# Reordering TensorE's turn in a pipelined LM block: dense products between the transposes, the scores and the scan products

## Time and profile before

| | |
|---|---|
| median of 3 runs | 1468.62 us (1467.59 to 1469.27) |
| the profiled execution | 1464.07 us, its span 1462.2 us |
| mean granted clock of PE | 0.915 |
| PE busy | 1184.4 us, 81% |
| DVE busy | 1160.4 us, 79% |
| ACT busy | 757.9 us, 52% |
| POOL busy | 819.6 us, 56% |
| HBM | 63 GB/s over the span |

### The profile page before, as it was taken

One profiled execution on the slowest core, in us unless ns is written; L12 is line 12 of the kernel. 1 busy time (PEld: TensorE's weight loads), 2 busy tenths in 40 slices (PEclk: granted clock), 3 DMA queues, 4 the chain that ended last, 5 costly groups with the idle time before them and its releaser, 6 DMA issues. The chain is left out here.

```text
span 1462.2 us, 25531 instructions
## 1 busy us (share of the span) xinstructions
PE 1184.4 (81%) x7199; PEld 814.6 (56%) x7206; DVE 1160.4 (79%) x2087; ACT 757.9 (52%) x1108; POOL 819.6 (56%) x2326
## 2 busy tenths in 40 slices
PE   0694043498989898989898989899999999898767
PEld 0352021357575756676767666666666675757444
DVE  4899933678888889888888989888888978878268
ACT  4667352354637373828273737473736555451247
POOL 7860027574757566575757575757575757560100
PEclk9999996599989899989899989998989989999889
DMA  9999400000001010101000000000000000000015
GB/s 367 408 407 425 160 23 16 12 19 16 23 10 31 1 32 3 30 6 26 10 22 16 16 16 16 16 16 16 16 16 16 16 16 16 18 17 1 0 42 188
DMA packets 62068, 92.22 MB, mean 63 GB/s; under 512 B 9101, under 2 KB 55010, under 8 KB 57554
## 3 DMA queue, kind: packets, MB, share of 16 engines
q1 hardware_dynamic: 58386, 82.10, 15.8%
q0 software_dynamic: 3072, 8.39, 1.5%
q10 hardware_dynamic: 576, 1.31, 0.2%
HBM read 81.29 MB, written 10.49 MB: 63 GB/s over the span
## 5 line engine op out<-in xcount | busy, mean ns | idle before, releaser
L747 POOL TENSOR_TENSOR stp<-Gs,X 128x32 f32<-128x32 f32 x1024 | 290.4, 284 | 263.1 <-ACT X L722 152.9
L749 POOL TENSOR_TENSOR Gs<-Gs,stp 128x32 f32<-128x32 f32 x1024 | 286.6, 280 | 80.3
L1048 PE MATMUL bank<-mT,w_fc 128*128 128x512 f32 x512 | 236.3, 599 | 7.9 <-ACT mT L1036 7.9
L604 PE MATMUL bank<-xT,w_in 128*128 128x512 f32 x512 | 235.8, 610 | 8.0 <-DVE uT L851 8.0
L1067 PE MATMUL bank<-w_fc,gl 128*128 128x256 f32 x1024 | 236.5, 379 | 0.0
L1067 PEld LDWEIGHTS bank<-w_fc,gl 128*128 128x128 f32 x1024 | 193.4, 190 | 59.8 <-issue 37.5
L837 ACT ACTIVATE uT<-bank,cols 128x512 f32<-128x512 f32 x64 | 49.5, 778 | 276.6 <-PE bank L604 276.6
L604 PEld LDWEIGHTS bank<-xT,w_in 128*128 128x128 f32 x512 | 97.7, 196 | 117.6 <-issue 107.1
L1048 PEld LDWEIGHTS bank<-mT,w_fc 128*128 128x128 f32 x512 | 95.7, 192 | 100.1 <-issue 94.7
L952 PE MATMUL bank<-MT,utok 128*64 128x128 f32 x1024 | 112.1, 408 | 45.5 <-DVE MT L938 45.4
L851 DVE SCALAR_TENSOR_TENSOR uT<-bank,cols,uT 128x500 f32<-128x500 f32 (+1 forms) x192 | 135.1, 736 | 3.0 <-ACT uT L837 0.7
(11 more groups left out here) (171 smaller groups left out, 1899.8 us busy)
## 6 DMA issues: line engine op xcount, KB each, us to landing
ring<-in_table SPq DMA_DIRECT2D x32, 1536.0 KB, 20.9
d_rep<-d_rows SPq DMA_DIRECT2D x128, 64.0 KB, 2.7
out<-res SPq DMA_DIRECT2D x16, 512.0 KB, 2.9
b_rep<-bc_rows SPq DMA_DIRECT2D x128, 32.0 KB, 1.8
c_rep<-bc_rows SPq DMA_DIRECT2D x128, 32.0 KB, 1.8
w_fc<-in_w_fc SPq DMA_DIRECT2D x2, 1024.0 KB, 8.8
w_in<-in_w_in ACTq DMA_DIRECT2D x1, 1088.0 KB, 5.2
h<-in_table,ids POOLq DMA_INDIRECT x64, 9.8
```

The source lines that it names most:

```text
L604: last = pe.matmul(dst, w_in[:, k, c0:c1], xT[:, k, :], start=(k == 0), stop=(k == KD - 1))
L747: pool.tensor_tensor(stp[:], Gs[:, t, ::-1, :], X2[:, t, :, :], ALU.mult).then_inc(rec.sem, 1)
L749: pool.tensor_tensor(Gs[:, t + 1, :, :], Gs[:, t, :, :], stp[:], ALU.add).then_inc(rec.sem, 1)
L1048: last = pe.matmul(pj[n % 4][:, :], w_fc1[:, k, n * P:(n + 1) * P], mT[:, k, :], start=(k == 0), stop=(k == KD - 1))
```

## The change

No arithmetic is changed. It moves pieces in PE's and DVE's orders, puts the scores in other banks, and splits `dve_gate`:

- PE: the transposes of u stand before tiles 5 and 6 of fc2, the first scores before tile 7. The four banks of scores are tb[0], tb[1], pj[2], pj[3], so the scores wait for the gate (`z_ready`) and for all of `gelu`, and the second head group's first pair waits for three masks in place of two (pj[2] must have been read). Tiles 0 and 1 of `pe_u` stand between the second scores and the second scan products, tiles 2 and 3 behind them. `pe_out` takes over the wait for `h2_ready`.
- DVE: `dve_layer_norm` goes from before `dve_inverse` to behind `dve_mean3`; `dve_row_stats` goes to before the first masks; `dve_h2` to behind them; `dve_stats3` to behind the gates; the skip of tiles 0 and 1 is before the second masks and their gate behind; the first half of the convolution is before `dve_bc`.

```
--- before.py
+++ after.py
@@ -822,8 +822,8 @@
                 dve.scalar_tensor_tensor(q, rm[:, :, hg * SC:(hg + 1) * SC].rearrange("p t s -> p s t"), DOWN80, q,
                                          ALU.mult, ALU.mult).then_inc(q_ready.sem, 1)
 
-        def pe_u(pe, g):
-            for f in range(UT):
+        def pe_u(pe, g, tiles):
+            for f in tiles:
                 if since(g):
 
                     pe.wait_ge(gate1.sem, gate1.at(g - 1, f + 1))
@@ -907,15 +907,16 @@
                 dve.scalar_tensor_tensor(xl[:, j, :], rows(g, j), rs1[:, bass.ds(g * G + j, 1)], out_b[:],
                                          ALU.mult, ALU.add).then_inc(xl_ready.sem, 1)
 
-        score_bank = (sbk[0], sbk[1], tb[0], tb[1])
+        score_bank = (tb[0], tb[1], pj[2], pj[3])
 
         def pe_scores(pe, g, hg):
             if hg == 0:
                 pe.wait_ge(k_ready.sem, k_ready.at(g))
                 pe.wait_ge(utok_ready.sem, utok_ready.at(g))
+                pe.wait_ge(z_ready.sem, z_ready.at(g))
                 if since(g):
 
-                    pe.wait_ge(h2_ready.sem, h2_ready.at(g - 1))
+                    pe.wait_ge(gelu.sem, gelu.at(g - 1))
             else:
                 pe.wait_ge(m_ready.sem, m_ready.at(g, 4))
             pe.wait_ge(q_ready.sem, q_ready.at(g, hg + 1))
@@ -940,12 +941,8 @@
                               ALU.mult).then_inc(m_ready.sem, 1)
 
         def pe_scan_out(pe, g, hg, pair):
-            if hg == 0 and pair == 0:
-
-                pe.wait_ge(z_ready.sem, z_ready.at(g))
-                if since(g):
-                    pe.wait_ge(gelu.sem, gelu.at(g - 1))
-            pe.wait_ge(m_ready.sem, m_ready.at(g, 4 * hg + 2 * pair + 2))
+
+            pe.wait_ge(m_ready.sem, m_ready.at(g, 4 * hg + (4 if hg and pair else 2 * pair + 2 + hg)))
             for j in range(G):
                 for hh in (2 * pair, 2 * pair + 1):
                     head = 4 * hg + hh
@@ -953,11 +950,13 @@
                                      utok[:, j, head * HP:(head + 1) * HP], MT[hh][:, j, :], start=True, stop=True)
             last.then_inc(y_mm.sem, 1)
 
-        def dve_gate(dve, g, tiles):
+        def dve_skip(dve, g, tiles):
             for f in tiles:
                 dve.wait_ge(y_mm.sem, y_mm.at(g, f + 1))
                 dve.scalar_tensor_tensor(uT[:, f, :], uT[:, f, :], c("d_skip", f), pj[f][:, :], ALU.mult, ALU.add) \
                     .then_inc(gate1.sem, 1)
+
+        def dve_gate(dve, g, tiles):
             for f in tiles:
                 dve.wait_ge(gate1.sem, gate1.at(g, f + 1))
                 dve.wait_ge(z_ready.sem, z_ready.at(g))
@@ -965,6 +964,8 @@
 
         def pe_out(pe, g):
             pe.wait_ge(m_ready.sem, m_ready.at(g))
+            if since(g):
+                pe.wait_ge(h2_ready.sem, h2_ready.at(g - 1))
             for n in range(2):
                 for j in (2 * n, 2 * n + 1):
                     for f in range(UT):
@@ -1154,22 +1155,29 @@
                 for n in range(FT + LEAD):
                     if third and n < FT:
                         pe_fc1(pe, m, n, p if second else None)
-                    if second and n == FT + 1:
+                    if second and n == FT:
                         pe_u_T(pe, p, g if first else None, 0)
                         pe_u_T(pe, p, g if first else None, 1)
+                    if second and n == FT + 1:
+                        pe_u_T(pe, p, g if first else None, 2)
+                        pe_u_T(pe, p, g if first else None, 3)
+                    if second and n == FT + 2:
+                        pe_scores(pe, p, 0)
                     if third and n >= LEAD:
                         pe_fc2(pe, m, n - LEAD)
                     if first and n == 6:
                         pe_ss(pe, g)
                 if second:
-                    pe_u_T(pe, p, g if first else None, 2)
-                    pe_u_T(pe, p, g if first else None, 3)
-                    for hg in range(HG):
-                        pe_scores(pe, p, hg)
-                        pe_scan_out(pe, p, hg, 0)
-                        pe_scan_out(pe, p, hg, 1)
-                if first:
-                    pe_u(pe, g)
+                    pe_scan_out(pe, p, 0, 0)
+                    pe_scan_out(pe, p, 0, 1)
+                    pe_scores(pe, p, 1)
+                if first:
+                    pe_u(pe, g, (0, 1))
+                if second:
+                    pe_scan_out(pe, p, 1, 0)
+                    pe_scan_out(pe, p, 1, 1)
+                if first:
+                    pe_u(pe, g, (2, 3))
                 if second:
                     pe_out(pe, p)
             turns(pe, turn)
@@ -1235,34 +1243,31 @@
                     dve_d(dve, g)
                 if second:
                     dve_keys(dve, p)
-                    dve_layer_norm(dve, p)
                     dve_inverse(dve, p)
                     dve_queries(dve, p)
-                if third:
-                    dve_h2(dve, m)
-                if second and nxt:
-
-                    dve.wait_ge(quant.sem, quant.at(g + 1))
+                if nxt:
+                    dve_row_stats(dve, g + 1)
                 if second:
                     for hh in range(4):
                         dve_mask(dve, p, 0, hh)
                 if third:
+                    dve_h2(dve, m)
+                if second:
+                    dve_skip(dve, p, (0, 1))
+                    for hh in range(4):
+                        dve_mask(dve, p, 1, hh)
+                    dve_gate(dve, p, (0, 1))
+                    dve_skip(dve, p, (2, 3))
+                    dve_gate(dve, p, (2, 3))
+                if third:
                     for j in range(G):
                         dve_stats3(dve, m, j)
+                    dve_mean3(dve, m)
                 if second:
-                    dve_gate(dve, p, (0, 1))
-                    for hh in range(4):
-                        dve_mask(dve, p, 1, hh)
-                if nxt:
-                    dve_row_stats(dve, g + 1)
-                if second:
-                    dve_gate(dve, p, (2, 3))
-                if third:
-                    dve_mean3(dve, m)
-                if first:
+                    dve_layer_norm(dve, p)
+                if first:
+                    dve_conv_u(dve, g, (0, 1))
                     dve_bc(dve, g)
-                if first:
-                    dve_conv_u(dve, g, (0, 1))
                 if nxt:
                     dve_rms_rows(dve, g + 1)
                 if second:
```

More of the change, by code:

```diff
@@ L1249, in turn @@
                 if third:
+                    dve_h2(dve, m)
[7 more added lines that the diff above has]
+                if third:
                     for j in range(G):
                         dve_stats3(dve, m, j)
+                    dve_mean3(dve, m)
                 if second:
-                    dve_gate(dve, p, (0, 1))
-                    for hh in range(4):
-                        dve_mask(dve, p, 1, hh)
-                if nxt:
-                    dve_row_stats(dve, g + 1)
-                if second:
-                    dve_gate(dve, p, (2, 3))
-                if third:
-                    dve_mean3(dve, m)
-                if first:
-                    dve_bc(dve, g)
+                    dve_layer_norm(dve, p)
                 if first:
                     dve_conv_u(dve, g, (0, 1))
+                    dve_bc(dve, g)
                 if nxt:
```

## The result

The kernel after takes 1427.99 us (median of 4 runs, 1426.39 to 1431.43) against 1468.11 for the kernel before beside it: a ratio of 0.9736 (95% interval 0.9706 to 0.9766), 2.6% faster. I had forecast 1485, slower, with a range from 1450. Both the direction and the range were wrong.

What follows compares the result with a forecast made beforehand. It took PE's scan waits and low clock, then PE's and DVE's chains ending together before fc1, as the bound. 14.4 us for the turns + 3.5 - 1.7 took 1464.1 to 1480; with 4.5 for the median, 1485 us, range 1450 to 1509.

Steps and rivals of the forecast that it cites:

- The waits of the old scan: PE's waits of 0.88 and twice 1.41 us around the scan, 3.7 us a turn, all covered by the new order.
- part 1: PE from fc1 to the last scan product: 28.74 us plus the moved work, 43.3 us, running dense.
- full-clock sum of 69.0: The new turn before clock loss, 43.3 + 25.7 = 69.0 us; the old turn was taken as 69.0 too.
- Part 2: From the last scan product to the next fc1: DVE's queue of 20.8 us plus 4.9, 25.7 against 24.8 before.
- PE's three new waits: New idle of PE before the gate's tiles 2 and 3 and the MLP's transposes: 0.8, 1.2 and 2.9 us.
- Part 3: The clock falls in PE's new idle before fc1, costing 2.2 us a turn, between 0 and 3.1.
- The turn: One loop turn, fc1 to fc1: 69.0 + 2.2 = 71.2 us against 70.17, +14.4 us over 14 turns.
- The ends: Turns outside the 14: turn 1 costs +3.5 us, turn 16 gains 1.7 us.
- A: Clock holds before fc1, which loses under 1.0 us a turn; turn 69.0, total 1454 us; chance 0.17.
- rival B: Clock falls in the scan's stretch as well as before fc1: turn 72.9, total 1509 us; chance 0.16.
- C: No change: fc1's clock loss is 1 us, half of turn 17's; total 1469 us; chance 0.12.
- D: DVE's tail is hidden and PE's own work bounds: turn 64.4, total 1390 us; chance 0.05.

Runs made afterwards that it cites:

- b_fill: Kernel before with filler products of constants (512 columns) in PE's three scan waits, nothing reordered: 1452.08 us, ratio 0.9921.
- a_ln_old: Kernel after with layer_norm back in its old place before dve_inverse: 1409.34 us, ratio 0.9631 to the kernel before.
- a_tail: Kernel after with bc moved behind the row statistics, and stats3 and mean3 before the second masks: 1401.12 us, ratio 0.9564 to the kernel before.
- a_gap_fill: Kernel after with five 256-column fillers in PE's wait before the MLP's transposes: 1414.15 us, ratio 0.9671 to the kernel before.
- b_fill_half: Kernel before with filler products of 256 columns in PE's three scan waits, nothing reordered: 1437.24 us, ratio 0.9826.
- a_u_behind: Kernel after with all four tiles of u behind the scan products, none between: 1411.48 us, ratio 0.964 to the kernel before.
- each half of the change: Kernel before with the new banks and only PE's new order: 1484.32 us, ratio 1.0142; or only DVE's: 1484.36 us, ratio 1.0134.
- a_ln_early: Kernel after with layer_norm moved before dve_keys: 1427.13 us, ratio 0.9758 to the kernel before.
- a_u_one: Kernel after with one tile of u before the second scan products, three behind: 1411.4 us, ratio 0.9649 to the kernel before.
- a_u_one_gap: Kernel after with one tile of u before the second scan products and five 256-column fillers before the MLP's transposes: 1409.56 us, ratio 0.9626 to the kernel before.

## Why the prediction was wrong

- **The waits of the old scan, and that the new order covers them:** right. There is no wait from fc1 to the last scan product, and 41.9 us between them where I had 43.1 to 43.3.
- **The step that failed: the price of the scan products in part 1.** I took 3.28 us for each 32 instructions from 779.28 to 782.56, and noted in the same text that the clock falls in that stretch. That price was one of the low clock. At full clock it is 1.90 (759.31 to 761.21), and b_fill shows the same 1.97 in the old order. Twice 1.38 is 2.8 us a turn. I had let a full-clock sum of 69.0 contain half-clock lengths, and then found it confirmed by an old turn of 69.0, which was one of the five short ones and had the low clock in its own scan. So the clock's gain never appeared in my sum, only its loss, and that made the forecast a slower kernel.
- **Smaller terms of part 1:** each score group took 1.94 and not 1.75, the tile of fc2 behind scores 1.93 and not 1.73, two tiles of u 3.63 and not 3.44. Together 0.8 us the other way.
- **Part 2, DVE's tail:** 21.1 measured, 20.8 forecast; that it sets the next fc1 was right, and a_ln_old and a_tail bear it out. PE's three new waits were forecast as 0.8, 1.2 and 2.9 and came as 0.75, 1.00 and 2.46.
- **Part 3, the clock before fc1:** it fell where I said, but cost 0.7 to 0.9 us a turn (a_gap_fill), not 2.2. This is the second term that was mis-sized. Turn 17 waits 9.49 us in one piece; here two tiles of the gate stand in the wait, and fc1's first 16 instructions pay 0.56 and not 1.9, with 0.3 more ahead of them (from rms, 789.86, to the next fc1, 795.13, it is 5.3 and not 4.9). Why so little of the low stretch reaches fc1 stays open. The range 0 to 3.1 did hold it. I had also written that single waits of 1.41 us were enough to bring the clock down in the old scan; b_fill_half waits 1.26 and 0.68 us there and a_u_behind 2.01, and the clock stays at 1.00 in most scans of the first and in some of the second. The wait alone does not decide it.
- **The turn:** 71.2 less 2.8, plus 0.8, less 1.3 for the clock (0.9 in place of 2.2), plus 0.3 for the tail is 68.2, which is what turns 5 to 13 measure. The mean of 67.96 is lower for the short turn 15.
- **The ends:** I had +1.8, measured are -3.9 and -2.5. In turn 1 I expected the last scan product 3.5 us later and it came 2.7 earlier (297.45 to 294.74): its second scan products took 1.97 at 292.77 in place of 3.68, another length of the low clock. The way from there to fc1, for which I had no term, got 1.2 shorter. And the 4.5 us that I added between the profiled execution and the median were 1.2. Of the 57 us by which the median was off, the turns are 45, the ends 8 and this 3.
- **The rivals:** A's condition was met as I had written it (fc1 lost 0.56 us, under 1.0), though the clock did not hold; its price of 1454 rests on the same wrong 69.0. The scan's clock in rival B did not fall. C had the loss ahead of fc1 nearly right, and not the time. No rival held the case that the new order wins back the length of the scan products; the result lay between A and D.

Some things stay open. How the gain splits between clock and orders is not known: b_fill_half shows 1.5 us a turn from the clock in the old order, with fillers in it, and each half of the change is a loss, so the parts do not add. What the new banks do by themselves was not run. Whether transposes count less than products for the clock, no run here tells. And no run takes POOL's addition out of DVE's way, so what that is worth is read from times alone.

## What to carry to other kernels

Before a length from a trace goes into a sum, read the clock that PE was granted in that very stretch, and price moved products at the clock they will have; small products that look bound by issue may be halved by it as well. Check that the turn taken as the measure is a typical one. A dense order on one engine may pay only with the order on the other that keeps it fed: here each half lost 1.3 to 1.4%. Then follow the chain from the last moved product to the next start of the loop, and take out of it whatever can stand in a wait elsewhere; that gave another 1.8%.

## What the runs showed that I had not expected

- The scan's instructions (weights of 64 columns, 128 columns moved) take 1.97 us per 32 at a granted clock of 1.00 and 3.68 at 0.50, nearly the full factor of two.
- Useless products in a wait can pay: three that took 2.77 us in a wait of 1.41 made the kernel before 0.8% faster, fillers that fit 1.7%.
- POOL's long additions stop DVE. An instruction of DVE that starts while the second one (L1081 before, L1082 after) runs ends about its own length behind it: L770 in b_fill_half, L775 in a_tail, and in a_ln_early the four instructions of L907 (3.68 in place of 1.67). The Trainium skill, "SBUF — State Buffer", section "SBUF: two separate sides", says that GpSimd and a VectorE instruction with two SBUF inputs contend for one pair of ports as an exclusive lock, and the later one waits for the whole instruction. The three cases agree: 739.49 + 1.1 is the 740.57 at which L770 ends, 726.13 + 1.0 the 727.10 of L775, and 735.77 + 1.5 the 737.23 of L907. It costs 1.7 to 2.2 us each time, and no piece has to be moved for it: in b_fill_half DVE's order is that of before. In the kernel after L770 takes 1.23 and L775 1.09 in nearly every turn, so the change's order misses the addition; a_u_one, a_u_one_gap and a_tail, which shorten the turn, run into it.
